# A four-layer decoder on one core: the fp4 rounding moved beside the first projection, and statistics moved into the tails of the self-attentions

## The chip, the cores and the metric

One NeuronCore of one Trainium2 chip runs the whole program in a single launch. The metric is the device time of one execution in microseconds (us), as the median of several executions. The engines are PE (TensorE, matrix products), DVE (VectorE), ACT (ScalarE), POOL (GpSimd) and SP (SyncE, which issues the DMAs). Each runs its own queue of instructions in order and waits on semaphores.

## The reference

The input x has 4 sequences of 256 tokens and 256 features. Four layers follow, each adding an attention, a cross-attention (or a recurrence) and a feed-forward block to x, each behind a layer norm without gain. What bears on the change:

```python
x = x + L0_attn(layernorm(x), Wq, Wk, Wv, Wo)
x = x + L0_xattn(layernorm(x), ctx)
x = x + L0_ffn(layernorm(x), up_kernel, ...)
...
x = x + L2_attn(layernorm(x), ...)
x = x + L2_xattn(layernorm(x), ctx)
...
x = x + L3_attn(layernorm(x), ...)
x = x + L3_wkv(w, u, layernorm(x), ctx)
x = x + L3_ffn(x)
```

L0_attn has rotary positions, tanh-capped scores and a causal mask; L2_attn (32 heads of 8) and L3_attn (16 of 16) are causal; L3_wkv is running maxima, exponentials and running sums. Both kernels of L0_ffn are rounded to fp4 first. The rounding takes every group of 32 weights, finds the power of two that belongs to its largest magnitude, divides by it, rounds the magnitude to one of 0, 0.5, 1, 1.5, 2, 3, 4, 6 (thresholds 0.25, 0.75, 1.25, 1.75, 2.5, 3.5, 5.0), and multiplies back with the sign. Two kernels of 256 x 1024 are rounded, 4096 numbers per partition.

## The kernel before, in words

The program is a row of blocks; a block ends when all engines have reached its end, so the slowest engine sets its length. Tokens lie on partitions in X (eight tiles of 128 tokens, in four groups g of two); HT holds the normed tokens turned, features on partitions.

**First projection** (`project`). All loads are issued at the start by `loads`. After the layer norm of `norm_steps`, PE works through 12 items n: for each, 128 output features of q or k for 512 tokens. It forms two products per item, one with the weights (q0, k0) and one with their columns swapped within each head (qp0, kp0), into banks 2 * (n % 2) and the next. DVE multiplies the first with the cosines (RC, L961) and the second with the sines (RS, L962), and POOL adds them (L973). RC and RS have two slots each, so DVE's item n waits for POOL's item n - 2. POOL begins by waiting for every load of the program (`b_in`, L969). PE then forms the eight V tiles (L936), and turns the context (L945), which ACT copies out (L980, L983).

**The rounding** (`quantise_fp4`) runs on DVE alone. The 4096 columns are eight pieces of 512; a piece is a chain of 17 instructions (L1162 to L1179), each behind the one before it. `beside_projection` deals five pieces out over items 2 to 11, 8 or 9 instructions behind the two rope multiplies of each item; `beside_attention` deals the other three out over the first attention. `turn_kernels` has PE turn the rounded kernels (L1245) at the start of the first cross-attention, and ACT copy them out (L1232).

**First attention** (`capped_attention`). 16 steps g (4 sequences b of 4 groups of heads). PE makes scores (L420), ACT tanh and exp (L483, L488), POOL masks (L509), PE multiplies with V and with ones (L441, L444), DVE copies the values out (L525). After a sequence's last step, DVE inverts the sums (L527) and spreads them (L532), POOL scales four tiles (L504) between its masks, and PE applies the output weights (L458) for two sequences inside the loop and two behind it. DVE adds to X (L520).

**The starts behind the three self-attentions.** `norm_steps` gives *measure* (statistics of a group, L288 and L291; where `pre` is set, an add of the output product to X comes first, L376), *root* (ACT, L324, behind a table load), *apply* (DVE, reciprocal and subtract-multiply, L295 and L298), *turn* (PE, L361) and *copy* (ACT, L329). All of it runs at the start of the block that follows: `shifted_attention` for the first cross-attention and for the third (`cross16`), and `wkv_scan` for the recurrence, whose DVE order is measures and applies of all four groups (`norm["vector"]`), then the running maxima (`gaps`, L2095). In the two grouped self-attentions (`shifted_attention` with `after`), PE's last work is the output product of the four groups (L352); DVE and ACT are then idle.

## Time and profile before

| | |
|---|---|
| median of 3 runs (lowest to highest) | 1392.82 us (1390.68 to 1394.52) |
| the profiled execution's own time | 1394.05 us |
| its span in the profile | 1392.3 us |
| mean granted clock of PE over the span | 0.953 |
| busy: PE, DVE, ACT, POOL | 1239.9, 817.3, 526.3, 329.8 us |
| first projection starts, ends | 14, 102.3 us |
| the weights to be rounded land at | 20.2 us (3.3 and 16.9 from issue) |
| first attention ends | 181.8 us |
| first cross-attention ends | 247.6 us |

The profile is of one execution; the span leaves out 1.8 us of its time. Busy time is given by engine, line and tile; an idle time is put down to the instruction that ended it. PE reaches 89% of the span, but most of the change lies in the first 250 us, where no single engine is full throughout, so the timeline of each stretch says more than the totals.

### The profile page before, as it was taken

The page shows a single profiled execution, that of the slowest core. Times are in us where ns is not written, and L with a number is a line of the kernel's source. Part 1 is how long each engine was busy: PE and PEld are TensorE (multiplying, and loading weights), DVE is VectorE, ACT ScalarE, POOL GpSimd, SP SyncE. Part 2 cuts the span into 40 slices and gives each one's busy share as a digit, 9 for nine tenths or more (in the row PEclk, how much of TensorE's full clock was granted, in tenths as well). Part 3 has the DMA queues.
Part 4 walks back from the last instruction along what each step waited for, and adds up shares of the span by engine and source line. Part 5 has one row for each costly group of instructions (what it writes and reads, how often), then busy time and mean ns, then how long its engine had stood idle before and what let it go on. Part 6 is the DMA issues. An engine that isn't in the chain of part 4 may idle for free. (4 is left out here: it accounts for less than half of the span.)

```text
span 1392.3 us, 23432 instructions
## 1 busy us (share of the span) xinstructions
PE 1239.9 (89%) x9322; PEld 744.2 (53%) x9334; DVE 817.3 (59%) x2109; ACT 526.3 (38%) x967; POOL 329.8 (24%) x364
## 2 busy tenths in 40 slices
PE   5678779788999899899998998999999999994898
PEld 2246554456854544556664544555555555663455
DVE  2887767757687344768766766343111126777955
ACT  1019335563524433544444545111111114445453
POOL 0225502100003100245542221232222223450200
PEclk9688899998999999999999999999999999996999
DMA  9000000000040030000000000123232210000000
GB/s 384 1 0 3 1 1 2 0 1 1 1 197 2 10 112 1 1 2 3 3 2 1 2 2 1 52 75 95 80 106 80 84 37 1 2 3 0 1 1 31
DMA packets 13340, 48.02 MB, mean 34 GB/s; under 512 B 1688, under 2 KB 4888, under 8 KB 12464
## 3 DMA queue, kind: packets, MB, share of 16 engines
q1 hardware_dynamic: 13232, 46.53, 10.0%
q8 instruction: 74, 1.21, 0.4%
q14 instruction: 34, 0.28, 0.1%
HBM read 45.37 MB, written 1.15 MB: 33 GB/s over the span
## 5 line engine op out<-in xcount | busy, mean ns | idle before, releaser
L821 ACT ACTIVATE PT<-PS 128x384 f32<-128x384 f32 (+1 forms) x320 | 153.2, 531 | 189.3 <-PE PS L631 138.4
L1930 PE MATMUL PS<-HT,WA 128*128 128x512 f32 x448 | 201.5, 593 | 2.4 <-DVE MO L2008 2.0
L2008 DVE TENSOR_TENSOR MO<-PS,AO 128x512 f32<-128x512 f32 x56 | 38.7, 690 | 205.9 <-ACT AO L1998 205.8
L1930 PEld LDWEIGHTS PS<-HT,WA 128*128 128x128 f32 x448 | 84.7, 190 | 87.7 <-issue 82.9
L1998 ACT ACTIVATE AO<-PS 128x512 f32<-128x512 f32 x56 | 33.3, 597 | 247.9 <-PE PS L1930 247.9
L757 DVE CUSTOM_DVE_ANT_0 junk<-PS,TRI 128x128 bf16<-128x128 f32 (+1 forms) x384 | 112.6, 352 | 4.0 <-PE PS L612 0.2
L1938 PE MATMUL PS<-WA,HO 128*128 128x256 f32 x448 | 105.6, 378 | 0.0
L1938 PEld LDWEIGHTS PS<-WA,HO 128*128 128x128 f32 x448 | 84.5, 189 | 34.7 <-issue 24.9
L240 PE MATMUL PS<-identb 128*128 128x512 bf16 x388 | 99.2, 394 | 3.2 <-PEq L584 1.2
L2063 POOL TENSOR_TENSOR HO<-MO,GR 128x512 f32<-128x512 f32 x44 | 57.8, 1314 | 168.7 <-PE PS L1938 168.7
L612 PE MATMUL PS<-KS,QM 32*128 32x128 f32 (+1 forms) x768 | 86.7, 347 | 7.5 <-DVE QM L791 6.6
L631 PE MATMUL PS<-QM,KS 32*128 32x256 f32 (+1 forms) x768 | 88.5, 347 | 0.0
L796 DVE RECIPROCAL OD<-OD 128x256 f32<-128x256 f32 x40 | 69.9, 1747 | 30.9 <-ACT OD L829 25.9
L859 POOL TENSOR_SCALAR_AFFINE_SELECT PT<-PT 128x512 f32<-128x512 f32 x96 | 60.8, 635 | 99.0 <-ACT PT L821 99.0
L869 POOL TENSOR_TENSOR OD<-OD 128x256 f32<-128x256 f32 x24 | 17.4, 726 | 272.6 <-DVE OD L796 272.6
L612 PEld LDWEIGHTS PS<-KS,QM 32*128 32x128 f32 x768 | 65.6, 184 | 30.2 <-DVE QM L791 16.6
L700 PE MATMUL PS<-PT,CST 128*32 128x256 f32 (+1 forms) x1280 | 75.4, 353 | 0.0
L929 PE MATMUL PS<-HT,WA 128*128 128x512 f32 x96 | 53.3, 721 | 19.2 <-DVE RS L962 19.2
L631 PEld LDWEIGHTS PS<-QM,KS 32*128 32x128 f32 x768 | 65.6, 184 | 1.9 <-issue 1.2
L240 PEld LDWEIGHTS PS<-identb 128*128 128x128 bf16 x388 | 36.4, 101 | 48.7 <-issue 17.0
L700 PE MATMUL PS<-PT,VM 128*32 128x256 f32 (+1 forms) x1024 | 58.3, 345 | 2.0 <-POOL PT L859 1.8
L1068 POOL TENSOR_TENSOR ROT<-RC,RS 128x512 f32<-128x512 f32 x16 | 20.3, 1270 | 149.0 <-DVE RS L1057 147.7
(323 smaller groups left out, 2412.8 us busy)
## 6 DMA issues: line engine op xcount, KB each, us to landing
WA<-w2f_in SPq DMA_DIRECT2D x28, 384.0 KB, 4.5
WA<-wl_in SPq DMA_DIRECT2D x1, 5137.0 KB, 16.0
GR<-gate_rows SPq DMA_DIRECT2D x20, 256.0 KB, 3.9
GB<-gate_rows SPq DMA_DIRECT2D x8, 512.0 KB, 7.4
WA<-wa_in SPq DMA_DIRECT2D x2, 1792.0 KB, 12.2
WB<-wb_in SPq DMA_DIRECT2D x1, 3208.0 KB, 18.4
WA<-wa_in SPq DMA_DIRECT2D x1, 2560.0 KB, 16.9
GR<-gate_rows SPq DMA_DIRECT2D x4, 448.0 KB, 4.0
```

The costliest lines, as they stand in the source:

```text
L240: pe.matmul(PS[:, bank, :].rearrange("p (a n) -> p a n", a=4), identb[:], identb[:].rearrange("p (a n) -> p a n", a=1).to_broadcast([P, 4, ...
L612: return pe.matmul(PS[:, s, m * T:m * T + n], queries(U, v)[rows, m * P:(m + 1) * P], keys(U, v)[rows, 0:n], start=True, stop=True, skip_g ...
L631: last = pe.matmul(bank, keys(U, v)[rows, n * P:(n + 1) * P], queries(U, v)[rows, lo:hi], start=n == 0, stop=r > 1, skip_group_check=True, ...
L700: last = pe.matmul(PS[at:at + 32, 7, what * T + lo:what * T + hi], lhs, src, start=what == 0 and v == 0 and n == 0, stop=v == r - 1 and n ...
L757: last = dve.tensor_tensor_reduce(junk[:, s, m * P:m * T + P], PS[:, s, m * T:m * T + (m + 1) * P], TRI[:, (1 - m) * P:T], 1.0, NEG, ALU.a ...
L796: dve.reciprocal(o, o).then_inc(S["at_inv"], 1)
L821: act.activation(PT[:, g % 3, st_slot(k), 0:W], PS[:, st_bank(g, k), 0:W], ACT.Exp, scale=scale).then_inc(S["at_exp"], 1)
L859: pool.affine_select(v, v, [[0, 4], [1, P]], ALU.is_ge, 0.0, base=0, channel_multiplier=-1).then_inc(S["at_masked"], 1)
L929: last = pe.matmul(PS[:, 2 * (n % 2) + half, :], wt[:, k, j * P:(j + 1) * P], HT[:, k, c * CH:(c + 1) * CH], start=k == 0, stop=k == KD - 1)
L1930: last = pe.matmul(PS[:, 2 * c + half, :], chunk(i, half)[:, k * P:(k + 1) * P], HT[:, k, c * CH:(c + 1) * CH], start=k == 0, stop=k == KD ...
L1938: last = pe.matmul(PS[:, 4 + t // 2, (t % 2) * D:(t % 2 + 1) * D], HO[:, c, j * P:(j + 1) * P], chunk(i, 2), start=i == 0 and t % 2 == 0, ...
L2063: pool.tensor_tensor(HO[:, c], MO[:, c], gate[:, c * CH:(c + 1) * CH], ALU.mult).then_inc(S["pool_mark"], 1)
```

## The change

1. *First projection.* One product per item in place of two; the swapped columns are made on DVE by a stream shuffle (L980) of the product, the cosines follow on DVE (L981), and POOL now does the sines (L991) and the sum (L995). Four banks and four slots of RC and RS are used. The weights qp0 and kp0 are no longer loaded. POOL waits for the constants only, and for `b_in` at its end. The V tiles come between the items (V tile n - 2 behind item n).
2. *The rounding.* All eight pieces run beside the projection. The magnitudes come from ACT (L1227, behind each V copy); the largest of each group of 32 for all pieces from eight reductions (L1201) beside items 1 to 3, and the powers once for all (L1206 to L1212). Item m + 4 has piece m: DVE scales it (L1218) and makes four of the seven comparisons (L1241), POOL the other three, each a 0 or a step height in bf16. PE sums the seven with an identity in bf16 (L1249), two items later; DVE puts sign and power together (L1232) and multiplies (L1255). PE turns the result as bf16 (L1274) at the last item, and ACT copies it out.
3. *Tails.* The measures of groups 0 to 2 and their roots, with the adds ahead of them where there are any, run at the end of the three self-attention blocks (`MEASURED = 3`), in the first attention behind the adds to X. The blocks behind them start with the applies. In the scan the maxima come between the applies.

```diff
 def project(w, nq, hd, QT, KT, V, kernels, arrived, first):
...
-            RC = st.enter_context(nc.sbuf_tensor("RC" + tag, [P, 2, CH], F32))
+            RC, RS = tmp("RC", [P, BUF, CH]), tmp("RS", [P, BUF, CH])
...
                     for n, (a, _, j, c) in enumerate(work):
-                        if n >= 2:
-                            pe.wait_ge(S["rope_sin"], d["rope_sin"] + n - 1)
-                        for half, wt in enumerate((a, ap)):
+                        if n >= 4:
+                            pe.wait_ge(S["rope_pair"], d["rope_pair"] + n - 3)
+                            pe.wait_ge(S["rope_cos"], d["rope_cos"] + n - 3)
...
+                        kernels["tensor"](pe, n, NW)
 
                 def _(dve):
...
+                        dve.stream_shuffle(RS[:, n % BUF], ps, PAIR[hd]).then_inc(S["rope_pair"], 1)
+                        dve.tensor_tensor(wide(RC[:, n % BUF]), wide(ps), cos.to_broadcast([P, nchunk, T]),
+                                          ALU.mult).then_inc(S["rope_cos"], 1)
+                        kernels["vector"](dve, n, NW)
 
                 def _(pool):
+                    pool.wait_ge(S["const_in"], 16)
+                    for n, (_, dst, j, c) in enumerate(work):
+                        pool.wait_ge(S["rope_pair"], d["rope_pair"] + n + 1)
+                        pool.tensor_tensor(wide(RS[:, n % BUF]), wide(RS[:, n % BUF]), sin.to_broadcast([P, nchunk, T]),
+                                           ALU.mult).then_inc(S["rope_sin"], 1)
...
+                        pool.tensor_tensor(dst[:, j, c * CH:(c + 1) * CH], RC[:, n % BUF], RS[:, n % BUF], ALU.add).then_inc(S["rope_sum"], 1)
+                        kernels["beside"](pool, n, NW)
                     pool.wait_ge(S["b_in"], 64)
-                    for n, (_, _, dst, j, c) in enumerate(work):
...
 def quantise_fp4():
...
+        def steps_of(eng, m, lo, hi, name):
+            eng.wait_ge(S["q_scaled"], m + 1)
+            if m >= 2:
+                eng.wait_ge(S["q_summed"], m - 1)
+            for j in range(lo, hi):
+                eng.tensor_scalar(at["steps"][:, m % 2, j, :], at["scaled"][:, m % 4], STEPS[j][0], STEPS[j][1], ALU.is_ge, ALU.mult).then_inc(S[name], 1)
+
+        def summed(pe, m):
...
+            for j in range(len(STEPS)):
+                last = pe.matmul(PS[:, 6 + m % 2, :], identb[:], at["steps"][:, m % 2, j, :], start=j == 0, stop=j == len(STEPS) - 1)
...
+        def kept(dve, m):
+            dve.wait_ge(S["q_summed"], m + 1)
+            dve.wait_ge(S["q_signed"], m + 1)
+            dve.tensor_tensor(rounded(m), PS[:, 6 + m % 2, :], at["signed"][:, m % 2], ALU.mult).then_inc(S["q_kept"], 1)
...
 def capped_attention(...):
...
                         dve.tensor_tensor(v, outs(b), v, ALU.add).then_inc(S["cap_added"], 1)
+                        if b < MEASURED:
+                            dve.wait_ge(S["cap_added"], b + 1)
+                            after["measure"](dve, b)
...
-                        beside(dve, g, NQ)
...
 def shifted_attention(...):
...
-                    if head is not None:
-                        head(pe, 0)
-                    elif norm is not None:
+                    if norm is not None:
                         warm(pe, 0, 24)
...
-                        for g in range(3):
-                            norm["measure"](dve, g)
-                            if g:
-                                norm["apply"](dve, g - 1)
+                        for g in range(MEASURED - 1):
+                            norm["apply"](dve, g)
...
+                    if after is not None:
+                        for b in range(MEASURED):
+                            after["measure"](dve, b)
...
 def wkv_scan(left, norm):
...
-                    norm["vector"](dve)
+                    norm["apply"](dve, 0)
+                    norm["measure"](dve, 3)
+                    norm["apply"](dve, 1)
                     gaps(0)
+                    norm["apply"](dve, 2)
                     gaps(1)
+                    norm["apply"](dve, 3)
...
-                    norm["scalar"](act)
+                    norm["copy"](act, 0)
+                    norm["root"](act, 3)
+                    norm["copy"](act, 1)
                     exps(0)
+                    norm["copy"](act, 2)
                     exps(1)
+                    norm["copy"](act, 3)
```

How DVE's order reads in the first projection. Before, the rows between two pairs of rope multiplies (L961, L962) are half a piece of the rounding:

```order
L961 TENSOR_TENSOR RC<-PS,CST 128x512
L962 TENSOR_TENSOR RS<-PS,CST 128x512
L1162 TENSOR_SCALAR H<-WA 128x512
L1163 TENSOR_REDUCE H<-H 128x16
L1164 TENSOR_SCALAR H<-H 128x16
L1166 TENSOR_SCALAR H<-H 128x16
L1167 TENSOR_SCALAR H<-H 128x16
L1168 RECIPROCAL H<-H 128x16
L1169 TENSOR_TENSOR H<-H 128x512
L1171 TENSOR_SCALAR H<-H 128x512
L961 TENSOR_TENSOR RC<-PS,CST 128x512
L962 TENSOR_TENSOR RS<-PS,CST 128x512
```

With the change, an item in the middle (scale, comparisons of this piece, result and sign of earlier ones, then the next item's shuffle and cosines):

```order
L980 STREAM_SHUFFLE RS<-PS 128x512
L981 TENSOR_TENSOR RC<-PS,CST 128x512
L1218 TENSOR_TENSOR H<-H,SM 128x512
L1241 TENSOR_SCALAR IND<-H 128x512 x4
L1255 TENSOR_TENSOR WA<-PS,SP 128x512
L1232 SCALAR_TENSOR_TENSOR SP<-WA,SM 128x512
L980 STREAM_SHUFFLE RS<-PS 128x512
L981 TENSOR_TENSOR RC<-PS,CST 128x512
```

Half a piece per item has become a whole piece per item, and a piece is seven instructions here where it was 17.

How DVE's order reads at the start of the scan. Before, the last adds, measures and applies ahead of the first running maximum (L2095):

```order
L288 BN_STATS stats<-X 128x6 x2
L291 BN_AGGR mom<-stats 128x2 x2
L295 RECIPROCAL rstd<-std 128x2
L298 TENSOR_SCALAR H<-X,mom,rstd 128x256 x2
L376 TENSOR_TENSOR X<-PS,X 128x512
L288 BN_STATS stats<-X 128x6 x2
L291 BN_AGGR mom<-stats 128x2 x2
L295 RECIPROCAL rstd<-std 128x2
L298 TENSOR_SCALAR H<-X,mom,rstd 128x256 x2
L295 RECIPROCAL rstd<-std 128x2
L298 TENSOR_SCALAR H<-X,mom,rstd 128x256 x2
L2095 SCALAR_TENSOR_TENSOR O<-VEC,HT 128x256 x2
```

With the change (the first row here stands directly behind the small constants of the block):

```order
L297 RECIPROCAL rstd<-std 128x2
L300 TENSOR_SCALAR H<-X,mom,rstd 128x256 x2
L378 TENSOR_TENSOR X<-PS,X 128x512
L290 BN_STATS stats<-X 128x6 x2
L293 BN_AGGR mom<-stats 128x2 x2
L297 RECIPROCAL rstd<-std 128x2
L300 TENSOR_SCALAR H<-X,mom,rstd 128x256 x2
L2172 SCALAR_TENSOR_TENSOR O<-VEC,HT 128x256 x2
L2175 TENSOR_TENSOR EV<-HT,O 128x2x256
```

One add and measure and two applies are left ahead of the first maximum; the other three adds and measures stand in the block before.

## Rows read from the trace of the kernel before

**Rows 1.** Busy time by stretch: first projection, first attention (columns: busy us, instructions)
```profile
38.00:102.30 64.30, 47.16 (x112) 23.29 (x112) 61.48 (x105) 5.24 (x12) 15.20 (x11) 0.79 0.00 0
...
102.30:182.00 79.70, 64.68 (x832) 47.61 (x832) 55.53 (x107) 47.53 (x65) 40.28 (x48) 0.88 0.01 2
```

**Rows 2.** Timeline of the first projection, VectorE and GpSimd (start us, us)
```profile
18.83 0.69 DVE L961 TENSOR_TENSOR RC<-PS,CST 128x512 f32<-128x512 f32 x1 [5.84 <-PE PS L929]
...
36.27 2.48 POOL L973 TENSOR_TENSOR QT<-RC,RS 128x512 f32<-128x512 f32 x2 [35.76 <-DMA WB<-wb_in]
...
37.63 0.69 DVE L961 TENSOR_TENSOR RC<-PS,CST 128x512 f32<-128x512 f32 x1 [14.15 <-POOL QT L973]
...
63.37 0.68 DVE L961 TENSOR_TENSOR RC<-PS,CST 128x512 f32<-128x512 f32 x1
...
76.23 0.68 DVE L961 TENSOR_TENSOR RC<-PS,CST 128x512 f32<-128x512 f32 x1
```

**Rows 3.** Groups of instructions of one shape: busy us, mean ns, idle before
```profile
L1053 DVE STREAM_SHUFFLE RS<-PS 128x512 f32<-128x512 f32 x16 | 11.8, 737 | 0.0
...
L1068 POOL TENSOR_TENSOR ROT<-RC,RS 128x512 f32<-128x512 f32 x16 | 20.3, 1270 | 149.0 <-DVE RS L1057 147.7 <-DVE RC L1054 1.3
...
L2425 POOL TENSOR_SCALAR KSX<-CX,CST 128x512 f32<-128x512 f32 x8 | 6.1, 778 | 5.0 <-SPq L584 5.0
...
L859 POOL TENSOR_SCALAR_AFFINE_SELECT PT<-PT 128x512 f32<-128x512 f32 x96 | 60.8, 635 | 99.0 <-ACT PT L821 99.0
```

**Rows 4.** Timeline, rounding steps without and with GpSimd beside them
```profile
80.47 0.43 DVE L1171 TENSOR_SCALAR H<-H 128x512 f32<-128x512 f32 x1
...
84.86 2.15 DVE L1174 SCALAR_TENSOR_TENSOR H<-H 128x512 f32<-128x512 f32 x3
...
124.57 3.27 DVE L1174 SCALAR_TENSOR_TENSOR H<-H 128x512 f32<-128x512 f32 x3
...
126.22 5.23 POOL L509 TENSOR_SCALAR_AFFINE_SELECT PT<-PT 128x512 f32<-128x512 f32 x5
```

**Rows 5.** Timeline of TensorE in the first projection
```profile
77.57 8.83 PE L929 MATMUL PS<-HT,WA 128*128 128x512 f32 x16 [2.67 <-DVE RS L962]
```

**Rows 6.** The wait list of TensorE, then the timeline of the first attention
```profile
PE PS L441 <- POOL PT L509: 10.4, 3, 4.5
...
132.85 0.86 PE L444 MATMUL PS<-PT,CST 128*32 128x256 f32 x16
...
135.26 0.42 DVE L525 COPY QT<-PS 128x256 f32<-128x256 f32 x1
...
171.73 0.42 DVE L525 COPY QT<-PS 128x256 f32<-128x256 f32 x1 [0.28 <-PE PS L444]
```

**Rows 7.** Timeline at the start of the first cross-attention
```profile
192.47 1.13 PE L612 MATMUL PS<-CX,H 32*128 32x256 f32 x8 [4.05 <-ACT WA L1232]
...
201.49 1.08 ACT L821 ACTIVATE PT<-PS 128x512 f32<-128x512 f32 x2 [7.78 <-PE PS L640]
```

**Rows 8.** Timeline at the start of the third cross-attention
```profile
735.45 5.34 PE L240 MATMUL PS<-identb 128*128 128x512 bf16 x24 [0.33 <-PEq L584]
...
754.84 1.08 ACT L821 ACTIVATE PT<-PS 128x512 f32<-128x512 f32 x2
```

**Rows 9.** Timeline at the start of the scan
```profile
1252.37 7.07 PE L352 MATMUL PS<-WA,HT 128*128 128x256 f32 x32
...
1260.11 0.69 DVE L376 TENSOR_TENSOR X<-PS,X 128x512 f32<-128x512 f32 x1
...
1261.72 0.66 DVE L376 TENSOR_TENSOR X<-PS,X 128x512 f32<-128x512 f32 x1
...
1269.81 1.27 DVE L2095 TENSOR_TENSOR_SCAN O<-VEC,HT 128x256 f32<-128x256 f32 x2
...
1271.84 0.91 ACT L2176 ACTIVATE KEEP<-EV,nw 128x256 f32<-128x256 f32 x2
...
1276.04 1.27 DVE L2103 TENSOR_TENSOR_SCAN QN<-KEEP,EK 128x256 f32<-128x256 f32 x2 [2.32 <-ACT EK L2182]
```

More of the change, by code:

```diff
@@ L367, in tensor @@
                 turn(pe, g)
-        return dict(begin=begin, measure=measure, apply=apply, vector=vector, scalar=scalar, tensor=tensor, product=product, turn=turn, columns=columns, tokens=tokens)
+        return dict(begin=begin, root=root, copy=copy, measure=measure, apply=apply, vector=vector, scalar=scalar, tensor=tensor, product=product, turn=turn, columns=columns, tokens=tokens)
     def add_sums():
@@ L494, in _ @@
                         exp(2 * g + 1)
+                    for b in range(MEASURED):
+                        after["root"](act, b)
                 @block.gpsimd
@@ L841, in _ @@
                             copy((g - 1) // r)
+                    if after is not None:
+                        for b in range(MEASURED):
+                            after["root"](act, b)
                 @block.gpsimd
@@ L892, in shifted_attention, with project @@
                 done[name] += k
-    def project(w, nq, hd, QT, KT, V, arrived=None, first=None, beside=None):
+    def project(w, nq, hd, QT, KT, V, kernels, arrived, first):
         cos = cst(f"cos{hd}", 1)
@@ new lines, in quantise_fp4, with begin @@
+        at = {}
+        rounded = lambda m: piece(order[m]).bitcast(BF16)[:, 0:CH]
+        def begin(tmp):
+            at.update(scaled=H[:].rearrange("p (j t) d -> p j (t d)", j=4), signed=tmp("SP", [P, 2, CH]), steps=tmp("IND", [P, 2, 7, CH], BF16),
+                      small=tmp("SM", [P, 3, early * NG]))
+        STEPS = [(5.0, 2.0), (3.5, 1.0), (2.5, 1.0), (1.75, 0.5), (1.25, 0.5), (0.75, 0.5), (0.25, 0.5)]
+        OWN = 4
+        per = lambda j, m: at["small"][:, j, m * NG:(m + 1) * NG]
@@ new lines, in quantise_fp4, with turned_over @@
+        turn = {m + 4: m for m in range(early)}
+        begun = {m: n for n, m in turn.items()}
+        def turned_over(pe, g):
+            need = (1, 3, 1, 3, 5, 5, 7, 7)[g]
+            pe.wait_ge(S["q_kept"], need + 1)
+            if g >= 2:
+                pe.wait_ge(S["q_copied"], g - 1)
+            for j in range(4):
+                if g < 4:
+                    f = 4 * (g % 2) + j
+                    m, at0 = f // 2, f % 2 * 2 * P + g // 2 * P
+                else:
+                    f = 2 * (g - 4) + j // 2
+                    m, at0 = 4 + j % 2 + f // 4 * 2, f % 4 * P
+                last = pe.matmul(PS[:, 4 + g % 2, j * P:(j + 1) * P], rounded(m)[:, at0:at0 + P], identb[:], start=True, stop=True,
+                                 skip_group_check=True)
+            last.then_inc(S["q_turned"], 1)
@@ L1254, in build_decoder, with beside_pool @@
+        def beside_pool(pool, n, last):
+            if n in turn:
+                steps_of(pool, turn[n], OWN, len(STEPS), "q_steps_beside")
+        return dict(begin=begin, tensor=beside_tensor, vector=beside_vector, beside=beside_pool, scalar=beside_scalar, after=last_scalar)
     spare_row = ROW[:, R_AT["b_dn0"][0]:R_AT["b_dn0"][0] + R_AT["b_dn0"][1]]
```

303 lines of the change are left out of this document (151 added, 152 removed).

## The prediction

> **What bounds the kernel now.** I read the totals first, then the busy time of the first two stretches, then the timelines where they idle, the wait list of PE, and last the starts of the blocks behind the self-attentions. PE is 89% busy, but not here: in the first projection DVE works 61.5 of 64.3 us and PE 47.2 [rows 1]. Two things set that stretch. DVE's third item starts at 37.63 after 14.15 us of waiting for POOL, and POOL's first add starts at 36.27 because it waits for the program's last load [rows 2]. From there DVE needs 12.86 us for two items and a piece of the rounding (63.37 to 76.23 [rows 2]): five pieces, 64.3 us, end at 102. In the first attention PE waits three times, 10.4 us in all, for a mask of POOL [rows 6], and POOL is slow there because DVE rounds beside it [rows 4]. The starts behind the self-attentions are chains of DVE work in front of the first exponential or scan [rows 7 to 9].
>
> **The change, stretch by stretch.** Against the profiled execution's 1394.05 us, which is 1.2 us above the median of the runs.
>
> *First projection.* It starts at 14 as now. The first DVE work behind a product comes at 18.83 after eight records of products [rows 2]; the change needs four of them, so about 17. Items 0 to 3 give DVE four shuffles of 0.74 [rows 3] and four multiplies of 0.69 [rows 2], eight reductions, which I price like the multiply at 0.69, and four small steps with their waits, 1.6 together: 5.7 + 5.5 + 1.6 = 12.8, less some 0.1 of overlap for each of 16 neighbours, plus 0.5 of waiting for item 1's product: they end at 29.5. The rounding's weights are no limit: they land at 20.2 now, at item 1, with 768 KB more ahead of them.
>
> Items 4 to 11 carry a piece each. DVE alone: shuffle 0.74, cosines 0.69, result 0.69 (2.1 in all); scale 0.72 and sign 0.72 (the price of a step with two tensors, 2.15 / 3 [rows 4]) and four comparisons of 0.43 [rows 4], 3.15 in all. POOL alone: two multiplies or adds of 1.27 and three comparisons. No POOL comparison is in the trace; nearest is POOL's multiply-add by scalars of the same size, 0.78, with its mask, which compares and selects, at 0.635 below and the two-tensor operation, 1.27, above [rows 3]. I take 0.78: 4.9 per item.
>
> They slow each other. Three two-tensor steps of DVE took 2.15 alone and 3.27 with POOL at work, a factor of 1.52, and POOL's five masks beside them 5.23 instead of 3.2, a factor of 1.64 [rows 4]. The multiply out of PSUM took 0.69 beside POOL's add and 0.68 without [rows 2]. So I stretch 3.15 by 1.52 to 4.8 and leave 2.1 alone: 6.9, less about 0.4 for overlap, **6.5 us per item**; POOL then does 2.1 at full rate and 4.4 / 1.64 = 2.7 in the rest, 4.8, just its work. The Trainium skill says in "GPSIMD Engine Reference", section Key points, that GpSimd shares its SBUF interfaces with VectorE and that contention comes with instructions in a two-port mode or with two SBUF inputs. By that rule the reductions, shuffles and PSUM multiplies go free, as I sum them, and the sum is 6.5; by a plain reading of the slow stretch, where all DVE work is slowed by 1.5, it would be 7.6. The untouched 0.69 agrees with the rule.
>
> Without any slowing the item costs 5.0, and if POOL and the contending steps took strict turns 2.1 + 3.15 + 2.8 = 8.0. PE is behind neither: two products of two records at 0.55 [rows 5], a V tile of half that and seven bf16 products of 0.22 [rows 8] are 2.2 + 1.1 + 1.6 = 4.9 per item.
>
> Eight items of 6.5, less 2.2 for results and signs that the first two lack, end at 79.3. Behind them: POOL's lag, seven products, the last result and four turned groups that ACT copies one by one, about 6 us. The stretch ends at 85.3 instead of 102.3: **-17.0** (bounds -29 at 5.0 per item, -5 at 8.0).
>
> *First attention.* DVE has only its copies left. At each of the three waits the first mask behind the four scalings loses about 0.4 [rows 3, 4] and the scalings, by the same factor, an estimated 0.5: 2.7. Before the second wait DVE copied at 135.26 what PE had ready at 133.7 [rows 6]; that 1.5 goes too. PE's clock falls in these waits (mean 0.88 in the stretch [rows 1]); shorter waits give an estimated 0.8 back. Added are three measures. The second stands between the add and the copy of the last step, which starts at 171.73 with 0.3 us of slack [rows 6] and has the reciprocal, the scalings and two output products behind it; it costs 0.9 - 0.3 = 0.6. The others lie in waits. Sum **-4.4** (bounds -8 and 0).
>
> *First cross-attention.* Now scores wait for the turned kernels until 192.47, and the first exp comes at 201.49, 19.4 after the block's start at 182.1 [rows 7]. Without turns and measures the chain is: 24 warming products, 5.3 [rows 8]; scores 0.6; maxima 2.3; the last measure 0.9 and an apply 0.8; splitting 1.0; turning 0.4; the first maximum of the next unit 1.4; scores and shifted scores 2.4: 15.1. **-4.1** (bounds -6 and -2). The warming products now come first: without them it would be 3 us more.
>
> *Third cross-attention.* The same chain is bound by the warming products until 740.8 [rows 8], where DVE came free at 743.8. That is 2.4 less, the tail's last root gives 0.2 back; the first exp comes that much before 754.84 [rows 8]. **-2.2** (bounds -3.5 and 0).
>
> *Scan.* Between 1260.11 and the first maximum at 1269.81 stand four add-and-measure pairs of 1.6 (1260.11 to 1261.72) and four applies, 9.7 in all [rows 9], so 0.8 an apply. Left ahead of it are one pair and two applies, 3.3. The first relu then starts at 1265.3, behind the first gap, where it stood at 1271.84 behind two copies; the running sums wait for it (1276.04 with 2.32 of idling [rows 9]) and DVE is full behind them, so the whole shift counts. The three pairs in the tail lie beside the output product, 7.07 us of PE [rows 9]; the last root sticks out by 0.2. **-6.4** (bounds -7 and -4).
>
> Sum: 17.0 + 4.4 + 4.1 + 2.2 + 6.4 = 34.1 off 1394.05, or 1360; by the median 1359.
>
> **The rivals.**
> - *The two engines hardly hinder each other* (5.0 per item): 12 us less in the first stretch, 1348. For it: comparisons of one source are not the steps that rows 4 measured. Against it: DVE is full either way and POOL nearly so.
> - *Something holds an item for about 8 us*: strict turns on the memory ports, POOL comparisons of 1.27 instead of 0.78, or PE at its lower clock (its grant was 0.79 in this stretch [rows 1]; all records at the half rate would make 8). The stretch ends at 97: 1372.
> - *The tails pay nothing.* If statistics there push the block's end by what they save behind it, only the first stretch and the attention remain: 1373. Against it: in both grouped tails DVE idles beside 7 us of PE [rows 9].
> - *Slower: POOL's comparisons.* All three stand in POOL's queue ahead of the next sines, and PE, then DVE, wait for their sum. The other terms bring 17 us, so the stretch may end at 119, or 10.7 per item; with POOL's two multiplies stretched to 1.6 each, that is reached at 2.5 us per comparison, four times its mask [rows 3]. At 4 us an item takes 15.2 and the kernel 1429. The mask, which compares and selects 512 columns in 0.635 us, speaks against it. 
>
> **How the numbers follow.** The forecast, items of 5.7 to 7.2 us, has 0.68; light hindrance 0.10; 8 us per item 0.14; empty tails 0.05; slow comparisons 0.03. The forecast's own range is 1350 to 1369. The range 1345 to 1375 takes in most of the next three and leaves out about 0.1. About 0.3% of the time, 4 us, can be told from no change: faster 0.96, same 0.01, slower 0.03.
>
> **What would show it.** In the new profile: POOL's first rope work near 18, not 36; DVE items 6.5 us apart and DVE over 90% busy from 30 to 79; POOL's comparisons near 0.8 to 1.2; the first attention's start near 86; PE's waits for masks under 8 us; the first exp 15 us behind the start of the first cross-attention; the first running sum 10 us behind the scan's start, not 16. I am wrong if PE or POOL's queue, not DVE, ends the waits between items, if POOL's comparisons are over 1.3 us, or if a tail block grows by more than 1 us.

## The result, and the profile after

The changed kernel takes 1380.59 us (median of 7 runs, 1379.34 to 1385.46) against 1395.15 us of the kernel before beside it (7 runs, 1390.68 to 1400.27): a ratio of 0.9901, 95% interval 0.9886 to 0.9917. It is 14.6 us faster, where 34 were forecast, and 1380.59 lies outside the range of 1345 to 1375. The span of the profiled execution is 1378.8 us, 13.5 less than before, with PE's granted clock at 0.962.

Per stretch, from the starts and ends in the two traces:

| stretch | before | after | change | forecast |
|---|---|---|---|---|
| first projection, end | 102.3 | 106.7 | +4.4 | -17.0 |
| first attention, length | 79.8 | 75.0 | -4.8 | -4.4 |
| first cross-attention, start to first exp | 19.4 | 15.6 | -3.8 | -4.1 |
| third cross-attention, output product to first exp | 26.8 | 25.3 | -1.5 | -2.2 |
| scan, output product to first running sum | 23.7 | 17.6 | -6.1 | -6.4 |

These make -11.8. Four of five terms came out within 0.7 us of the forecast. The first has the wrong sign. The third row starts in the kernel before at an output product that the rows ahead of the prediction do not show:

```profile
728.05 7.07 PE L352 MATMUL PS<-WA,HT 128*128 128x256 f32 x32
```

Of the other 1.7 us of the 13.5, 1.6 lie in the rest of the third cross-attention. From its first exp to the end of the block it takes 78.6 us before and 77.1 after. The difference arises in the first 103 products behind the exp, before and then after (us, busy time of PE, PEld, DVE, ACT and POOL, granted clock, DMA share, GB/s):

```profile
754.84:764.90 10.06, 9.32 (x103) 4.99 (x104) 4.04 (x5) 4.34 (x8) 0.00 (x0) 0.83 0.01 2
```

```profile
748.96:757.40 8.44, 7.70 (x103) 4.35 (x103) 4.04 (x5) 4.34 (x8) 0.00 (x0) 1.00 0.01 2
```

The granted clock there was 0.83 before and 1.00 after. It does not follow the tails: the run with seven comparisons on DVE (below) has the same tails and takes 78.5 us for this part again. So these 1.6 us are not a sure gain of the change.

The busy time by stretch in the first projection of the changed kernel (us, times busy, granted clock, DMA share, GB/s):

```profile
14.00:30.00 16.00, 16.00 (x45) 8.64 (x45) 12.94 (x27) 4.21 (x9) 9.48 (x9) 1.00 1.04 417
30.00:100.00 70.00, 33.97 (x115) 16.00 (x116) 41.32 (x77) 8.40 (x16) 68.05 (x40) 0.81 0.04 18
```

The columns behind the stretch are PE, PEld, DVE, ACT, POOL. Where DVE was full [rows 1], POOL now is: 68.05 of 70 us, and DVE has only 41.32. POOL's timeline of the changed kernel shows both halves of the story (start, duration, engine and line, idle time ahead):

```profile
17.47 1.09 POOL L991 TENSOR_TENSOR RS<-RS,CST 128x512 f32<-128x512 f32 x1 [16.96 <-DVE RS L980]
...
50.54 6.63 POOL L1241 TENSOR_SCALAR IND<-H 128x512 bf16<-128x512 f32 x3
57.14 1.09 POOL L991 TENSOR_TENSOR RS<-RS,CST 128x512 f32<-128x512 f32 x1
58.31 1.26 POOL L995 TENSOR_TENSOR QT<-RC,RS 128x512 f32<-128x512 f32 x1
59.66 6.48 POOL L1241 TENSOR_SCALAR IND<-H 128x512 bf16<-128x512 f32 x3
```

POOL's first rope work comes at 17.47, where it stood at 36.27 [rows 2]: the wait for the last load is gone, as forecast. But three comparisons take 6.5 us, not 2.3, and from 50.54 to 59.66 one item takes 9.1. Everybody else waits for that. DVE in the same stretch, the list of PE's waits up to 107, and what stands behind POOL's last comparison:

```profile
59.10 2.18 DVE L1241 TENSOR_SCALAR IND<-H 128x512 bf16<-128x512 f32 x4 [3.77 <-PE PS L1249]
...
69.55 2.25 DVE L1241 TENSOR_SCALAR IND<-H 128x512 bf16<-128x512 f32 x4 [5.25 <-PE PS L1249]
```

```profile
PE PS L1249 <- POOL IND L1241: 35.7, 8, 8.6
```

```profile
100.75 3.15 PE L1249 MATMUL PS<-IND,identb 128*128 128x512 bf16 x7 [5.15 <-POOL IND L1241]
...
103.94 0.69 DVE L1255 TENSOR_TENSOR WA<-PS,SP 128x512 bf16<-128x512 f32 x1 [7.61 <-PE PS L1249]
104.20 2.25 ACT L1322 ACTIVATE WA<-PS 128x512 bf16<-128x512 f32 x4 [14.71 <-PE PS L1274]
...
106.72 1.28 ACT L488 ACT_TABLE_LOAD   x1 [0.27 <-PEq L926]
```

DVE waits for PE's sum, and PE eight times, 35.7 us, for POOL's comparisons: a chain that names DVE as the victim and PE as the messenger. The tail behind POOL is 6 us, as forecast.

In the first attention the waits for masks fall to half of [rows 6], now that DVE does no rounding beside them:

```profile
PE PS L446 <- POOL PT L516: 5.6, 3, 1.9
```

And the three starts, which answer to [rows 7 to 9]: of the first cross-attention its warming products and the first exp, of the third the output product and the first exp, of the scan the output product, the first running maximum and the first running sum.

```profile
181.70 5.34 PE L241 MATMUL PS<-identb 128*128 128x512 bf16 x24 [1.05 <-PEq L412]
...
197.31 1.08 ACT L827 ACTIVATE PT<-PS 128x512 f32<-128x512 f32 x2 [4.29 <-PE PS L649]
```

```profile
723.71 7.07 PE L354 MATMUL PS<-WA,HT 128*128 128x256 f32 x32
...
748.96 1.08 ACT L827 ACTIVATE PT<-PS 128x512 f32<-128x512 f32 x2
```

```profile
1244.91 7.07 PE L354 MATMUL PS<-WA,HT 128*128 128x256 f32 x32
...
1256.25 1.27 DVE L2172 TENSOR_TENSOR_SCAN O<-VEC,HT 128x256 f32<-128x256 f32 x2
...
1262.48 1.27 DVE L2180 TENSOR_TENSOR_SCAN QN<-KEEP,EK 128x256 f32<-128x256 f32 x2 [0.63 <-ACT EK L2263]
```

DVE's idle time before the first running sum fell from 2.32 to 0.63 us, and the first maximum comes 11.3 us behind the output product's start instead of 17.4.

### The profile page after: what moved, and what is told of

Read it like the earlier page. It is cut to its first block and busy times, and to the rows that moved or that the text cites. A ratio compares the mean times of both kernels' runs of the same rounds, so it can differ in the third digit from the quotient of the medians.

```text
span 1378.8 us, 23544 instructions
## 1 busy us (share of the span) xinstructions
PE 1227.6 (89%) x9359; PEld 736.8 (53%) x9374; DVE 775.3 (56%) x2053; ACT 531.5 (39%) x975; POOL 382.1 (28%) x400
## 5 line engine op out<-in xcount | busy, mean ns | idle before, releaser
L2007 PE MATMUL PS<-HT,WA 128*128 128x512 f32 x448 | 201.5, 593 | 2.4 <-DVE MO L2085 2.0
L241 PE MATMUL PS<-identb 128*128 128x512 bf16 x420 | 104.1, 387 | 4.6 <-PEq L593 1.5
L878 POOL TENSOR_TENSOR OD<-OD 128x256 f32<-128x256 f32 x24 | 17.4, 727 | 268.5 <-DVE OD L799 268.5
L241 PEld LDWEIGHTS PS<-identb 128*128 128x128 bf16 x420 | 39.0, 100 | 53.0 <-issue 17.4
L1931 DVE SCALAR_TENSOR_TENSOR HB<-HA,ROW,GB 128x512 f32<-128x512 f32 x40 | 30.1, 751 | 40.9 <-ACT HA L1866 36.1
## 6 DMA issues: line engine op xcount, KB each, us to landing
WA<-wl_in SPq DMA_DIRECT2D x1, 5137.0 KB, 15.6
```

Source lines behind the costliest of these rows:

```text
L241: pe.matmul(PS[:, bank, :].rearrange("p (a n) -> p a n", a=4), identb[:], identb[:].rearrange("p (a n) -> p a n", a=1).to_broadcast([P, 4, ...
L2007: last = pe.matmul(PS[:, 2 * c + half, :], chunk(i, half)[:, k * P:(k + 1) * P], HT[:, k, c * CH:(c + 1) * CH], start=k == 0, stop=k == KD ...
```

## The experiments

Two theories of the first projection are tested. *Price*: a POOL comparison costs 2.1 us, so POOL's queue sets the item. *Sharing*: the comparisons are only long, or DVE only slow, because both engines work at once, or PE's chain holds the item anyway, so it doesn't matter who compares. Beside them, two questions of bookkeeping: what the one moved wait was worth, and what the tails are.

### All seven comparisons on DVE

```diff
-        OWN = 4
+        OWN = 7
```

> All seven comparisons of a piece on DVE, none on POOL (the same values, the same sum). Theory 1 (a POOL comparison of 128x512 costs 2.1 us, and POOL's queue sets the items at 8.9 us): POOL keeps two operations of about 1.1 us per item and falls far behind nothing; DVE has 3.5 us of unchanged work and seven comparisons of 0.45 to 0.5 us, so items of 6.6 to 7.0 us; the first stretch ends between 84 and 89 instead of 106.7 and the kernel takes 1359 to 1364 us. DVE's idle time in front of its comparisons (20.8 us in the changed kernel) goes. Theory 2 (the engines share something, and the sum of the work counts, wherever it is done; or PE's chain holds an item for 8 us): items stay at 8 us or more, the stretch ends behind 98, 1372 to 1381 us.

Measured: 1364.43 us, ratio to before 0.9795 (0.9774 to 0.9816). The price theory holds, half a us beyond its upper end. Busy time of DVE and POOL in that run, and one item on its timeline:

```profile
30.00:85.00 55.00, 32.23 (x119) 15.69 (x121) 54.73 (x102) 8.28 (x16) 21.46 (x16) 0.87 0.05 23
```

```profile
42.73 1.09 POOL L991 TENSOR_TENSOR RS<-RS,CST 128x512 f32<-128x512 f32 x1 [3.70 <-DVE RS L980]
...
43.08 1.29 DVE L1218 TENSOR_TENSOR H<-H,SM 128x512 f32<-128x512 f32 x1
...
43.90 1.59 POOL L995 TENSOR_TENSOR QT<-RC,RS 128x512 f32<-128x512 f32 x1
...
44.40 3.38 DVE L1241 TENSOR_SCALAR IND<-H 128x512 bf16<-128x512 f32 x7
...
51.48 3.39 DVE L1241 TENSOR_SCALAR IND<-H 128x512 bf16<-128x512 f32 x7
```

DVE is full (54.73 of 55 us), the item is 51.48 - 44.40 = 7.1 us, and the next block starts at 89.98, 16.7 us earlier. Moving three comparisons back to the engine that had been full in the kernel before gained more time than the whole change. The item is a little over the expected 6.6 to 7.0: DVE's scaling (L1218) takes 1.29 us, not 0.68. In the profiled execution the first attention is longer: 78.4 us against 75.0, with the same work at a lower clock. Its second part in this run, then in the changed kernel:

```profile
130.00:168.40 38.40, 32.63 (x340) 24.04 (x332) 14.52 (x41) 13.90 (x21) 11.39 (x18) 0.88 0.01 1
```

```profile
146.70:181.70 35.00, 29.21 (x336) 22.00 (x329) 14.51 (x41) 13.74 (x20) 11.20 (x18) 0.98 0.01 1
```

The granted clock there was 0.88 instead of 0.98: 3.4 of the 16.7 us are given back in this execution. It is the slowest of the four of this version (1368.98 us; the others took 1362.34 to 1365.28, at a granted clock of 0.965 to 0.967 over the span instead of 0.961), and the medians differ by 16.2 us, so the others need not have lost it. What set the clock lower is not settled. The early end of the projection alone does not: with the next block at 91.07 (two multiplications on POOL, below) the attention takes 74.9 us, and with the next block at 100.07 (bare comparison on POOL) 78.5.

### Six on DVE, one on POOL

`OWN = 6` in the same place.

> Six comparisons on DVE, one on POOL (the same values). Theory 1 (2.1 us for each POOL comparison): POOL has 2.4 + 2.1 = 4.5 to 5 us per item, DVE 3.5 us and six comparisons of 0.5 to 0.58, 6.4 to 7.0 us per item, so about the same as with all seven on DVE, within 3 us, 1357 to 1364 us; the single POOL comparison stays at 1.9 to 2.2 us. If the 2.1 us came from three in a row hindering DVE and POOL mutually, the single one would fall towards 1 us. Theory 2 (shared work or PE's chain): 1372 us or more.

Measured: 1367.33 us, ratio 0.9819 (0.9799 to 0.9838), 3 us above what theory 1 gave and well below theory 2. The single comparison on POOL in that run:

```profile
L1241 POOL TENSOR_SCALAR IND<-H 128x512 bf16<-128x512 f32 x6 | 13.2, 2192 | 0.0
```

It costs 2.19 us alone as well as three in a row. The next block starts 3.6 us later than with seven on DVE: POOL's one comparison makes the other six longer, 3.86 us for the six, where all seven took 3.39 without it. That hindrance was not in the expectation. POOL's price is not made by DVE either: the last two comparisons of the changed kernel run from 96.80 to 100.61 with DVE idle, 1.9 us each.

### What makes the price

Three runs change POOL's three instructions alone. Two multiplications by the same scalars:

```diff
-eng.tensor_scalar(steps, scaled, STEPS[j][0], STEPS[j][1], ALU.is_ge, ALU.mult)
+eng.tensor_scalar(steps, scaled, STEPS[j][0], STEPS[j][1], ALU.is_ge if lo == 0 else ALU.mult, ALU.mult)
```

> The changed kernel with POOL's three steps of each piece as two multiplications (by the same two scalars) instead of comparison and multiplication, same tiles, same types; their values are then not the steps of the rounding. If the comparison as an operation is what costs, they fall to about 0.8 us each (the multiply-add by scalars of the kernel before: 0.78), POOL has 5 us per item, DVE goes on without waiting and this is the case that was forecast: items of 6.5 us, stretch end at 85 to 88, 1359 to 1363 us. If it is the output in bf16 or the form of the instruction, they stay at 1.9 to 2.2 us, items at 8.9 and the time at 1378 to 1383 us.

The comparison without the multiplication by the height:

```diff
-eng.tensor_scalar(steps, scaled, STEPS[j][0], STEPS[j][1], ALU.is_ge, ALU.mult)
+eng.tensor_scalar(steps, scaled, STEPS[j][0], None, ALU.is_ge)
```

> The changed kernel with POOL's three steps as a bare comparison, without the multiplication by the height (the heights of these three steps are left out). If the comparison costs what the instruction takes, 1.9 to 2.2 us remain and the time is 1378 to 1383 us; if each of the two operations takes its share, 1.0 to 1.2 us remain, POOL has 5.8 us per item, DVE no longer waits, 1362 to 1368 us.

The output in f32 (`wide` is a scratch tile):

```diff
-eng.tensor_scalar(at["steps"][:, m % 2, j, :], ..., ALU.is_ge, ALU.mult)
+eng.tensor_scalar(at["wide"][:, j - lo, :], ..., ALU.is_ge, ALU.mult)
```

> The changed kernel with POOL's three comparisons written as f32 into tiles that nobody reads, and zeros summed in their place (these steps are left out of the rounding). If the conversion to bf16 in the output costs, they fall from 2.1 to about 0.8 to 1.3 us and the time to 1359 to 1368 us. If not, 1.9 to 2.2 us and 1378 to 1383 us.

Measured: 1364.46, 1378.07 and 1381.86 us (one run each; their values are not the rounding's). POOL's group in each from 40 to 80 us, in this order (busy us, mean ns):

```profile
L1241 POOL TENSOR_SCALAR IND<-H 128x512 bf16<-128x512 f32 x18 | 12.6, 709 | 1.0
```

```profile
L1244 POOL TENSOR_SCALAR IND<-H 128x512 bf16<-128x512 f32 x15 | 25.7, 1725 | 0.8
```

```profile
L1244 POOL TENSOR_SCALAR WIDE<-H 128x512 f32<-128x512 f32 x14 | 29.0, 2077 | 0.7
```

The output's type is nothing (2.08 against 2.06 us). The bare comparison still takes 1.73 us, nearer the first expectation, though under its 1.9. Two multiplications take 0.71. This looked like the operation itself, so two more runs put other operations in, one line each:

```diff
+                elif j == 4: eng.tensor_scalar(to, of, 1e30, h[1], ALU.is_ge, ALU.mult)
+                elif j == 5: eng.tensor_scalar(to, of, -1.0, h[1], ALU.is_ge, ALU.mult)
+                elif j == 6: eng.tensor_scalar(to, of, h[0], h[1], ALU.max, ALU.mult)
```

> The changed kernel with POOL's three steps of a piece made different operations on the same tile, one line each: comparison with 1e30 (never true), comparison with -1 (always true), maximum, each times the height (these steps of the rounding are replaced). If the 2.06 us come from branches on the data, the two comparisons without a change of outcome are well under it or differ from each other by over 0.3 us; if each element costs the same whatever its value, both take 1.9 to 2.2 us. Maximum: about 0.7 us if only comparisons that produce a 0 or 1 are dear, about 2 us if every operation that has to choose is.

```diff
+                elif j == 4: eng.tensor_scalar(to, of, h[0], None, ALU.mult)
+                elif j == 5: eng.tensor_scalar(to, of, h[0], h[1], ALU.mult, ALU.is_ge)
+                elif j == 6: eng.tensor_scalar(to, of, h[0], h[1], ALU.add, ALU.min)
```

> The same with one multiplication alone, multiplication then comparison, and addition then minimum (these steps of the rounding are replaced). The single multiplication takes 0.6 to 0.75 us, hardly less than the two in one instruction (0.71): the second arithmetic operation is nearly free. Multiplication then comparison: 1.9 to 2.2 us if the comparison costs wherever it stands, under 1.5 us if only its place ahead of another operation did. Addition then minimum: 0.7 us or about 2 us, as for the maximum.

Measured: 1382.40 and 1377.52 us (one run each). The groups, from 40 to 90 us, are in the first run never true (L1245), always true (L1247), maximum (L1249); of the second one multiplication (L1245), multiplication and comparison (L1247), addition and minimum (L1249):

```profile
L1247 POOL TENSOR_SCALAR IND<-H 128x512 bf16<-128x512 f32 x6 | 13.2, 2205 | 0.5
L1245 POOL TENSOR_SCALAR IND<-H 128x512 bf16<-128x512 f32 x6 | 12.5, 2089 | 0.5
L1249 POOL TENSOR_SCALAR IND<-H 128x512 bf16<-128x512 f32 x5 | 9.7, 1943 | 0.0
```

```profile
L1249 POOL TENSOR_SCALAR IND<-H 128x512 bf16<-128x512 f32 x6 | 12.0, 1997 | 0.0
L1247 POOL TENSOR_SCALAR IND<-H 128x512 bf16<-128x512 f32 x6 | 12.0, 1994 | 0.5
L1245 POOL TENSOR_SCALAR IND<-H 128x512 bf16<-128x512 f32 x6 | 10.4, 1741 | 0.5
```

An outcome that never changes costs as much as one that does: no branch on the data is seen. The surprise is the last line: one multiplication takes 1.74 us where two take 0.71. So it is not the comparison that is dear. Every form tried takes 1.7 to 2.2 us, except multiply-multiply here and the multiply-add of [rows 3]; those two pairs seem to have a fast way of their own. My expectation for the single multiplication (0.6 to 0.75) was wrong. The Trainium skill, "GPSIMD Engine Reference", section "Elementwise — side-by-side cycle accounting", gives about 1.8 cycles per element, 769 ns for 512 elements, as the best case of an unrolled loop without branches, and some 12 cycles where it branches on data. The 0.78 us agree with the first, and the 0.71 lie 8% below it. The second, at the page's clock of 1.2 GHz, makes an estimate of 5.1 us, and nothing here takes that; the 2.06 us lie between.

### How the two engines hinder each other

With cheap POOL instructions (two multiplications) the run is the case that the prediction summed: POOL's price 0.71 for my 0.78. It gave 1364.46 us (one run), not 1359, and DVE's item was 7.2 us, not 6.5. Its DVE and POOL instructions on the line of the comparisons (minimum, median, maximum ns):

```profile
L1241 DVE TENSOR_SCALAR IND<-H x4: 826/830/1375, 52.1 to 54.9; 128x512 bf16<-128x512 f32 x4
L1241 POOL TENSOR_SCALAR IND<-H x3: 669/675/781, 53.3 to 54.6; 128x512 bf16<-128x512 f32 x3
```

And the same line of the run with seven comparisons on DVE, where the only company is POOL's rope add:

```profile
L1241 DVE TENSOR_SCALAR IND<-H x40: 412/414/1375, 39.9 to 79.8; 128x512 bf16<-128x512 f32 x40
```

A comparison of DVE takes 0.414 us; beside POOL's multiplications 0.83, beside its add 1.375. That is no stretching by one factor. The ends of the single instructions show one engine waiting until the other's instruction is over: in the item from 52.08, POOL's multiplications end at 53.93, 54.68 and 55.42, and DVE's last three comparisons 0.27 to 0.29 us behind each. The turns are not strict, though: the two engines get through one instruction each in 0.75 us, less than the 0.675 + 0.414 that full durations in turn would take. The item shown above (seven on DVE) has it in the open: POOL's sines run from 42.73 to 43.82, DVE's scaling is issued at 43.08 and ends at 44.37, 0.55 behind them; POOL's add is issued at 43.90, into the scaling, and ends at 45.49, 1.1 behind that; DVE's first comparison then waits for the add. DVE loses 0.6 + 0.96 us per item so. The Trainium skill, "SBUF — State Buffer", section "SBUF: two separate sides", says the same: the pair of ports that both share is an exclusive lock, held for the whole instruction, for DVE against GpSimd where DVE has a two-port mode or two sources in SBUF. The trace agrees for POOL's products, adds and multiplications. It does not for POOL's comparisons: in the changed kernel DVE's four take 1.84 to 2.25 us beside them, 0.4 to 0.8 over the 1.43 that four in a row take with POOL idle (in the run with three signs on ACT, below), while POOL's last 2.06 us each. DVE's scaling, with two sources in SBUF, takes its own 0.67 us at 54.65, in the middle of POOL's three comparisons (50.54 to 57.17).

If it is a lock, moving DVE's two-source step away from the add should not help. That was the next run. Its expectation says that the comparisons lose nothing beside the add; the single durations above (1.375 us for the first of seven) show that this was a misreading.

```diff
             if n == 3:
                 powers(dve)
+                scaled(dve, 0)
             if n in turn:
                 m = turn[n]
-                scaled(dve, m)
                 steps_of(dve, m, 0, OWN, "q_steps")
+                if m + 1 < early:
+                    scaled(dve, m + 1)
```

> All seven comparisons on DVE, and the scaling of a piece (the product of two tensors in SBUF) moved in DVE's order: behind the comparisons of the piece before, not right behind the cosines. In the run with seven comparisons this scaling took 1.31 us beside POOL's add (0.68 in the changed kernel), the add 1.59 us (1.27), in every item; the comparisons lost nothing beside that same add. Theory (the two operations with two SBUF sources meet on something shared; which one DVE executes in that moment decides it): the scaling falls to 0.7 us, items from 7.05 to 6.4 us, the first stretch ends some 5 us earlier, 1358 to 1361 us. Rival (the loss goes to whatever DVE does beside the add, the comparisons now): items stay at 7.0 and the time at 1362 to 1367 us.

Measured: 1368.37 us, ratio 0.9800 (0.9778 to 0.9822), no different from 1364.43 by its interval and 1.4 us above the rival's range. The rival was right in its mechanism. The scaling is at its own price again, and the comparisons, now beside sines and add, have taken over the loss:

```profile
43.43 4.11 DVE L1241 TENSOR_SCALAR IND<-H 128x512 bf16<-128x512 f32 x7
47.46 0.68 DVE L1218 TENSOR_TENSOR H<-H,SM 128x512 f32<-128x512 f32 x1
...
50.48 4.13 DVE L1241 TENSOR_SCALAR IND<-H 128x512 bf16<-128x512 f32 x7
```

The item is 50.48 - 43.43 = 7.05 as before; seven comparisons went from 3.39 to 4.11 us.

### The one moved wait, alone

```diff
                 def _(pool):
-                    pool.wait_ge(S["b_in"], 64)
                     for n, (_, _, dst, j, c) in enumerate(work):
...
+                    pool.wait_ge(S["b_in"], 64)
```

> The kernel before, with one line moved: POOL's wait for the program's last load stands behind its adds of the first projection instead of ahead of them. Everything else (rounding, tails) is as before. Theory: that wait alone cost DVE 14 us (18.83 to 37.63 with 14.15 us of idling); without it POOL starts near 19 to 20 and DVE goes on at about 23 to 24, so the first stretch ends near 88 to 89 instead of 102.3 and the kernel takes 1380 to 1383 us: about the whole time of the changed kernel with none of its reordering. Rival: the wait is hidden behind the rounding's weights (they land at 20.2) or something else of that time, so DVE resumes no earlier than 30 and the kernel takes 1388 us or more.

Measured: 1383.30 us, ratio 0.9921 (0.9904 to 0.9937). DVE's third item, and the next block's start, in that run:

```profile
24.71 0.69 DVE L961 TENSOR_TENSOR RC<-PS,CST 128x512 f32<-128x512 f32 x1 [2.14 <-PE PS L929]
...
89.43 1.28 ACT L483 ACT_TABLE_LOAD   x1 [6.13 <-PEq L912]
```

DVE's third item starts at 24.71 instead of 37.63 [rows 2], and the stretch ends at 89.4 instead of 102.3: 12.9 us for one line, 11.2 of them left in the medians (1394.54 to 1383.30). The first attention of this execution is 1.9 us longer than before, 81.7 us at a granted clock of 0.83 where it was 0.88. That is three quarters of the gain of the whole change. It also says what the rest of the first part was worth as built: the stretch went from 89.4 to 106.7.

### The tails, undone

```diff
-    MEASURED = 3
+    MEASURED = 0
```

and at the starts of the blocks behind, and in the scan, the order of the kernel before.

> The changed kernel with its rounding, but without measures and roots in the self-attentions' tails: they stand behind them as in the kernel before. Theory (the tails pay what the changed trace shows: 6.1 us at the scan, 1.5 at the third cross-attention, some 2 of the 3.7 at the first, less 0.6 that the measures cost in the first attention): 9 us slower than the changed kernel, 1388 to 1392 us. Rival (the gain at the starts is only moved from the tails, or DVE makes it up later): within 3 us of the changed kernel, 1378 to 1383 us.

Measured: 1390.68 us, ratio 0.9974 (0.9960 to 0.9988), so 10 us slower than the changed kernel; its profiled span is 8.4 us longer. The scan's output product and first running sum, then those of the third cross-attention's start:

```profile
1247.16 7.07 PE L354 MATMUL PS<-WA,HT 128*128 128x256 f32 x32
...
1270.84 1.27 DVE L2182 TENSOR_TENSOR_SCAN QN<-KEEP,EK 128x256 f32<-128x256 f32 x2 [2.32 <-ACT EK L2261]
```

```profile
722.84 7.07 PE L354 MATMUL PS<-WA,HT 128*128 128x256 f32 x32
...
749.63 1.08 ACT L829 ACTIVATE PT<-PS 128x512 f32<-128x512 f32 x2
```

Both are back where they were before (23.7 and 26.8 us), so the tails pay 6.1 and 1.5 us there. The rest of the third cross-attention takes 78.6 us again, with the lower clock behind its first exp; as said above, that part can't be put down to the tails. The first cross-attention does not change: its first exp comes 15.6 us behind the start with or without the measures in the tail, behind the 5.34 us of warming products. All of its 3.8 us come from the turns of the kernels that left it; I had counted on about 2 from the tail. And the first attention is only 0.3 us longer for the measures.

### A version that beats both

ACT had 8.3 of 55 us of work in the projection, and DVE's load is what counts. So the steps of height 0.5 go to ACT as signs:

```diff
+        def signs(act, m):
+            act.wait_ge(S["q_scaled"], m + 1)
+            if m >= 2:
+                act.wait_ge(S["q_summed"], m - 1)
+            for j in range(OWN, len(STEPS)):
+                act.activation(at["steps"][:, m % 2, j, :], at["scaled"][:, m % 4], ACT.Sign,
+                               bias=at["below"][:, j - OWN:j - OWN + 1]).then_inc(S["q_steps_beside"], 1)
...
-                last = pe.matmul(..., identb[:], at["steps"]...)
+                last = pe.matmul(..., identb[:] if j < OWN else at["quarter"][:], at["steps"]...)
...
-            dve.tensor_tensor(rounded(m), PS[...], at["signed"][...], ALU.mult)
+            dve.scalar_tensor_tensor(rounded(m), PS[...], 0.75, at["signed"][...], ALU.add, ALU.mult)
```

> A version meant to beat both: four comparisons of a piece on DVE, the other three on ACT as signs of the piece less a threshold one step of f32 below (+1 or -1), summed with a quarter of the identity; the missing 0.75 is added by the step that multiplies the sum out of PSUM. POOL keeps only the rope. If DVE is what sets the items in the run with all seven comparisons on it (7.05 us, full from 30 to 85), three comparisons of 0.48 less give items of 5.6 us, 11 us off the first stretch and 1351 to 1356 us; ACT has 0.38 + 0.63 of its own and three of about 0.62, 2.9 us per item. If PE's chain or ACT's queue (signs in front of the copies that PE's V tiles wait for) sets the items then, they stay above 6.3 us and the kernel takes 1358 us or more.

Measured: 1361.60 us, ratio 0.9751 (0.9732 to 0.9771), where 1351 to 1356 was expected if DVE sets the items and 1358 or more if something else does. DVE is full until 70, its item 6.0 us, over the 5.6 expected. A comparison taken away saves 0.34 us (3.39 us for seven, 2.38 for four), not the 0.48 of the average over seven, in which the wait for the add was spread. The stretch ends at 85.3. With `OWN = 3` and 1.0 in the place of 0.75:

> As the run with three signs on ACT, but with four of the seven (all of height 0.5) on ACT and three comparisons on DVE. In that run DVE was full from 30 to 70 (39.76 of 40 us) with items of 6.0 us, and ACT had 18.5 of 40. If DVE still sets the items, one comparison of 0.48 us less in each of eight gives 5.5 us per item and 3 to 4 us off: 1357 to 1359.5 us. If PE sets them now (its sum of seven products and the turns at the lower clock behind 70), the stretch ends where it did, at 85, and the kernel takes 1360 to 1363 us.

Measured: 1359.98 us (5 runs, 1359.86 to 1360.72), ratio 0.9748 (0.9733 to 0.9763). An item of DVE is now 5.65 us:

```profile
49.95 0.72 DVE L980 STREAM_SHUFFLE RS<-PS 128x512 f32<-128x512 f32 x1
...
52.42 2.56 ACT L1248 ACTIVATE IND<-H,TH 128x512 bf16<-128x512 f32 x4 [2.31 <-DVE H L1218]
52.42 2.05 DVE L1241 TENSOR_SCALAR IND<-H 128x512 bf16<-128x512 f32 x3
...
55.60 0.72 DVE L980 STREAM_SHUFFLE RS<-PS 128x512 f32<-128x512 f32 x1
```

The next block starts at 83.39, 1.9 earlier than with three signs, where I had expected 3 to 4: behind 66 PE's sums and turns, not DVE, hold the end. By the two intervals three and four signs can't be told apart; both are some 20 us faster than the changed kernel. Most of that is what seven comparisons on DVE bring already (16.2 us by the medians); four signs on ACT add 4.5 to it. This is the best version run.

## Why the prediction was wrong

**First projection, -17.0 forecast, +4.4 measured: the step that failed.** Three of its steps held: POOL began at 17.5, DVE's item 4 at 29.1 (29.5 forecast, though the terms as written, 17 + 12.8 - 1.6 + 0.5, make 28.7), and the tail behind was 6.0 us. The step "nearest is POOL's multiply-add by scalars of the same size, 0.78 ... I take 0.78" failed. The measured mean is 2.06 us, and POOL's item 8.9 instead of 4.9. A row for one pair of operations was taken as the price of the instruction's form; the pair turned out to be the exception, as the single multiplication at 1.74 us shows. My other reason, that the mask "compares and selects" in 0.635 us, was no better: it is another instruction. What happened is the rival "POOL's comparisons", with its mechanism word for word (all three ahead of the next sines, PE and then DVE waiting for their sum), just short of the 2.5 us from which it would have made the kernel slower. I had given it 0.03, and nothing between 0.78 and 2.5 us had a share but the 1.27 in another rival. With an upper bound of 1.27 us from the two-tensor operation, the range itself was cut too short.

**The stretching by 1.52** also failed, but it is the smaller part: with POOL's instructions at 0.71 us, the forecast's own case, the kernel takes 1364.5 us, inside the range, with the next block starting at 91.1 for 85.3. The engines take turns, instruction by instruction (0.414 us become 0.83 and 1.375), so the item was 7.2 us. I had strict turns as a bound and priced them at 8.0. In the changed kernel itself it plays little part, since DVE idles there.

**First attention, -4.4 against -4.8**, and the cause holds: the waits for masks are 10.4 and 9.5 us in the two kernels that round beside them (before, and before with the later wait) and 5.6 in the changed kernel, in the one without tails and with seven comparisons on DVE, whatever the clock. The measures cost 0.3, not 0.6. That the sum fits to 0.4 us is in part luck: the same instructions took 75 us in some executions and 78.5 in others, with the granted clock.

**First cross-attention, -4.1 against -3.8.** The size is right (the terms as written make 19.4 - 15.1 = 4.3), the sharing of it was not: the tail brings nothing there.

**Third cross-attention and scan, -2.2 and -6.4 against -1.5 and -6.1.** Both shown by undoing the tails. The rival that tails pay nothing falls: they pay 10 us by the medians, of which the traces place 7.6 in these two starts.

So 16.2 of the 17.1 us forecast outside the first stretch came true, and 21.4 were lost in it. By the medians the change brings 14.6 us: the later wait alone brings 11.2, the tails 10.1, and so, if the parts simply add up, which no run tests, the rounding as divided between DVE and POOL, its gains in the attention and at the first cross-attention included, takes back 6.7.

## What to carry to other kernels

Before work goes to POOL, its price must be known for that very pair of operations; a neighbour of the same form and size can be off by 2.6. If no row shows it, the upper bound is a multiple, not the next row. Where DVE and POOL both work out of SBUF, don't stretch by one factor: the sum of the durations of what meets is an upper bound (1.09 us for 0.75 measured with multiplications), and it must be known for the very instruction too, since beside POOL's comparisons DVE lost little. Look first for an idle engine that the others don't hinder, here ACT: its signs took 0.70 to 0.72 us each beside both. A wait placed at the head of a queue can be worth more than a new algorithm: read why an engine's first instruction starts when it does.

## What was unexpected of the hardware

- POOL, 128x512, f32, one source with scalars: multiply-multiply 0.71 us; one multiply alone 1.74; one comparison 1.73; comparison-multiply 2.06; multiply-comparison 1.99; add-minimum 2.00; maximum-multiply 1.94. The type of the output (f32 or bf16) and the outcome of the comparison (never, always or sometimes true) make less than 0.2 us.
- DVE's comparison of 128x512 f32 into bf16 takes 0.414 us, five times less than POOL's, and waits out a POOL add that is under way (1.375 us then), but loses only about 0.1 to 0.2 us each beside POOL's comparisons.
- The same first attention took 75.0 us with a granted clock of 0.98 in its second part and 78.4 with 0.88, behind a projection that ended 17 us earlier. The earlier end is not enough: behind one that ended 15.6 us earlier it took 74.9. What sets it stays open.
- The third cross-attention behind its first exp took 77.1 or 78.6 us with the same instructions, at a granted clock of 1.00 or 0.83 in its first 8 to 10 us.
